# Only the first scatter group of a pair waits for TensorE's count

## The chip, the core and the metric

The kernel runs on one core of a Trainium2 chip. The engines are TensorE (PE), VectorE (DVE), ScalarE (ACT), GpSimd (POOL) and SyncE (SP), each with its own ordered list of instructions; sixteen DMA engines move data. The metric is the device time of one execution in microseconds; lower is better. The kernel before took 10546.78 us in the median of 3 runs (10500.81 to 10546.99).

## What is computed

Two layers over a graph of 12,500 nodes with 256 features and 212,500 edges, in float32. Cut to what bears on the changed stage:

```python
edge_index = jnp.stack([src, dst])
xn = _layernorm(x, axis=-1)
x = x + gcn_residual(xn, edge_index, edge_weight, ...) + linear_attention(xn, ...)
x = x + moe(_layernorm(x, axis=-1), router_w, w1, b1, w2, b2)   # 8 experts, top 2 combined
...
# moe: every expert is applied to every token
for e in range(8):
    h = gelu(tokens @ w1[e] + b1[e])
    y = h @ w2[e] + b2[e]
    out = out + combine[:, e:e+1] * y
# second layer: graph sum over the same edges, sorted anew, attention, feed-forward, slice attention
```

## The kernel before

The program is a row of stages, each with its own semaphores and a barrier behind it. The stage in question is `finish_layer0` (L1269). It takes the 100 tiles of 125 nodes in 50 pairs (`NP = 50`, `TE = 2` tiles each) and does, for each pair, the end of the graph layer and of the attention (the "front"), the 8 experts, and the norm and keys that the second layer needs (the "back").

The order is written out by hand. Every engine walks through 32 slots a pair; in slot n TensorE does one up product (`up`, L1955, tokens times a half of `w1[e]`, 4 matmuls with their weight loads) or one down product (`down`, L1965), and the front of the next pair and the back of the pair before are dealt out over the same slots. TensorE adds one to a semaphore behind each product. `up_done` counts the up products: 16 a pair, and product c of expert e in pair i brings it to i*16 + e*2 + c + 1. ScalarE waits for it and applies gelu (L1836), and adds to `up_kept`; TensorE's down product waits for that and adds to `dn_done`; VectorE waits for `dn_done` and adds the weighted result to `acc` (L1556), and adds to `dn_kept`, which TensorE awaits before it writes that bank again. There are two banks for up and two for down. So TensorE can run a few products ahead and then needs the others' counts, and these need its own. By the code TensorE gives 56 such counts a pair: 16 up, 16 down and 24 of front and back.

Beside this, GpSimd does a job that has nothing to do with the experts: it puts the edge records in a new order for the second layer. The records lie as 1,700 rows of 125 (`RPP = 34` rows a pair), and each row is one indirect DMA of 128 lanes with 12 bytes each, from `rec` to `sorted_recs` (L1472). Nobody in this stage reads `sorted_recs`; the next stage does, behind the barrier. SyncE loads `rec` and `pos` two pairs ahead (L1393, L1394) into four buffers, when GpSimd's `share_done` says that the buffer is free; the same SyncE queue loads `x` (L1431) and stores `x2` and `table1` (L1440, L1441).

GpSimd's 34 scatters of pair i are dealt into 8 groups (`NE = 8`; sizes 4, 4, 4, 5, 4, 4, 4, 5). Before group g it waits until `up_done` is at least (i-1)*16 + 2g + 1, that is until TensorE has done the first up product of expert g in pair i-1. Pair 0 has no such wait. Behind group 1 it waits until all scatters of the pair before have landed and gives SyncE `share_done`.

Of the kernel before, what the change touches and what calls it, by code (L numbers as in the profile page):

```python
# [1268 lines left out]
def finish_layer0(nc, k):  # L1269
# [11 lines left out]
    with ExitStack() as ctx:  # L1281
# [69 lines left out]
        S = Shared()  # L1351
# [30 lines left out]
        def by_fours(eng, run):  # L1382

            run(0, 0, 0)
            with eng.Fori(0, (NP - 2) // 4) as m:
                for q in range(1, 5):
                    run(m * 4 + q, q % 4, m + q // 4)
            run(NP - 1, (NP - 1) % 4, (NP - 1) // 4)
# [66 lines left out]
        @block.gpsimd  # L1455
        def _(eng):
            eng.memset(rec[:, :, :, :], 0).then_inc(spare_lanes, 1)
            for ring in range(4):
                eng.iota(pos[:, ring, :], [[LANES - P, RPP]], base=P * k.ROWS + ring % 2 * RPP * (LANES - P) - P,
                         channel_multiplier=1).then_inc(spare_lanes, 1)  # L1460
            eng.sem_inc(S.share_done, 1)

            def run(i, ring, turn):
                n = ring % 2
                eng.wait_ge(rec_in[ring], turn * 32 + 32)
                eng.nop(nofuse=True)
                for group in range(NE):
                    if not isinstance(i, int) or i > 0:
                        eng.wait_ge(S.up_done, (i - 1) * 16 + group * 2 + 1)
                        eng.nop(nofuse=True)  # L1470
                    for r in range(group * RPP // NE, (group + 1) * RPP // NE):
                        eng.indirect_dma_start(  # L1472
                            out=k.sorted_recs, out_offset=bass.IndirectOffsetOnAxis(ap=pos[:, ring, r:r + 1], axis=0),
                            in_=rec[:, ring, r, :], in_offset=None).then_inc(scattered[n], 16)
                    if group == 1 and (not isinstance(i, int) or i > 0):

                        eng.wait_ge(scattered[1 - n], (turn * 2 + (ring + 1) // 2) * (16 * RPP))
                        eng.sem_inc(S.share_done, 1)

            by_fours(eng, run)  # L1480
            for n in range(2):
                eng.wait_ge(scattered[n], 16 * RPP * (NP // 2))
                eng.nop(nofuse=True)
# [1848 lines left out]
```

## Time and profile before

| | us |
|---|---|
| median of 3 runs | 10546.78 |
| the profiled execution, its own time | 10519.44 |
| its span, first to last instruction | 10517.9 |
| TensorE matmul busy | 7714.1 (73%) |
| VectorE busy | 6440.3 (61%) |
| GpSimd busy | 5497.1 (52%) |
| ScalarE busy | 1737.1 (17%) |
| scatters, L1472, 1700 of them | 1717.7 busy |
| gathers of the graph sums, L879, 3600 of them | 3474.5 busy |

A reader should know: busy time is that of instructions, not of their waits. A matmul's end is modelled from its start. "Releaser" is what the profile takes to have ended an engine's idle time; "issue" means that nothing visible was waited for, and "remote" that the wait ended by a semaphore event for which the profile shows no instruction ending at that moment. A DMA_INDIRECT on POOL is the time in which GpSimd writes the descriptors, not that of the transfer. The granted TensorE clock was 0.82 of full speed over the span.

### The profile page before, as it was taken

The numbers are of one execution on the slowest core, as the hardware profiler recorded it, in microseconds if no ns is written. First come the engines' busy times: TensorE is split into PE (matmuls) and PEld (weight loads), VectorE is DVE, ScalarE is ACT, GpSimd is POOL, SyncE is SP. The second block draws the span as 40 slices with busy tenths as digits, with TensorE's granted clock in tenths as the row PEclk, the third lists the DMA queues.
The fourth block names the chain that finished last, engine by engine and source line by source line (L and its number), as shares of the span: only waits on it lengthen the run. The fifth ranks groups of instructions, "written<-read, shape, count | busy, mean of one in ns | idle before, by whom it ended". The sixth has DMA issues, their size and how long they took to land. (4 is left out here: it accounts for less than half of the span.)

```text
span 10517.9 us, 141328 instructions
## 1 busy us (share of the span) xinstructions
PE 7714.1 (73%) x33929; PEld 5693.3 (54%) x33929; DVE 6440.3 (61%) x22399; ACT 1737.1 (17%) x3475; POOL 5497.1 (52%) x5833
## 2 busy tenths in 40 slices
PE   4845565665665668888888888677777777777998
PEld 3634444444444446666666666455555555554667
DVE  5755555665655656666666666465565565555983
ACT  1110000000000013333333333111001101110221
POOL 2235555555555555665655666366565666654002
PEclk7767777777777779999999999788888888887999
DMA  1022222222222210000000000233232333322446
GB/s 48 29 87 80 79 82 82 82 83 80 84 83 81 82 56 15 16 16 15 17 16 15 17 16 15 58 91 93 89 91 89 93 93 90 92 86 77 127 114 195
DMA packets 451199, 724.74 MB, mean 69 GB/s; under 512 B 144672, under 2 KB 304613, under 8 KB 450193
## 3 DMA queue, kind: packets, MB, share of 16 engines
q0 software_dynamic: 235408, 493.09, 16.5%
q1 hardware_dynamic: 215180, 224.92, 7.4%
q14 instruction: 451, 3.69, 0.1%
q10 hardware_dynamic: 130, 2.55, 0.1%
q8 instruction: 30, 0.49, 0.0%
HBM read 611.64 MB, written 108.50 MB: 68 GB/s over the span
## 5 line engine op out<-in xcount | busy, mean ns | idle before, releaser
L879 POOL DMA_INDIRECT sum_gathered<-table,sum_idx x3600 | 3474.5, 965 | 2485.5 <-PE sum_agg_res L943 1180.7
L943 PE MATMUL sum_agg_res<-sum_gathered,sum_lay 125*125 125x256 f32 x7200 | 2480.2, 486 | 1315.7 <-DVE sum_lay L909 507.8
L943 PEld LDWEIGHTS sum_agg_res<-sum_gathered,sum_lay 125*125 125x125 f32 x7200 | 1576.2, 235 | 1961.2 <-DVE all_sums L928 1122.8
L928 DVE TENSOR_TENSOR all_sums<-all_sums,sum_agg_res 125x256 f32 x3600 | 1511.4, 420 | 1426.6 <-PE sum_agg_res L943 699.7
L1472 POOL DMA_INDIRECT sorted_recs<-fin_rec,fin_pos x1700 | 1717.7, 1010 | 1131.3 <-PE fin_ps_up L1961 481.3
L909 DVE TENSOR_SCALAR sum_lay<-all_lane,sum_dloc_now,sum_w_now 125x125 f32<-125x125 f32 x3612 | 1284.3, 356 | 53.2 <-issue 37.8
L1969 PE MATMUL fin_ps_dn<-fin_w,fin_hidden 128*125 128x256 f32 x3200 | 916.0, 422 | 84.6 <-DVE fin_acc L1556 60.3
L1961 PE MATMUL fin_ps_up<-fin_tokens_T,fin_w 128*128 128x250 f32 x3200 | 859.3, 396 | 73.0 <-ACT fin_hidden L1836 67.3
L1969 PEld LDWEIGHTS fin_ps_dn<-fin_w,fin_hidden 128*125 128x125 f32 x3200 | 633.6, 209 | 236.4 <-issue 134.5
L1556 DVE SCALAR_TENSOR_TENSOR fin_acc<-fin_ps_dn,fin_comb,fin_acc 125x256 f32<-125x256 f32 x800 | 381.4, 481 | 617.9 <-remote 355.8
L1961 PEld LDWEIGHTS fin_ps_up<-fin_tokens_T,fin_w 128*128 128x128 f32 x3200 | 603.0, 201 | 192.6 <-ACT fin_hidden L1836 99.2
L1836 ACT ACTIVATE fin_hidden<-fin_ps_up,fin_b 128x250 f32<-128x250 f32 x800 | 367.0, 470 | 1125.4 <-PE fin_ps_up L1961 590.3
L1043 DVE CUSTOM_DVE_ANT_0 sum_junk<-sum_src_hot,sum_ps_rank 125x100 f32<-125x100 bf16 x1700 | 335.9, 253 | 238.1 <-DMA table<-all_sums 226.5
L1124 PE MATMUL sum_ps_rank<-sum_src_hot,sum_edges_after 125*125 125x100 bf16 x1700 | 209.8, 257 | 349.1 <-DVE sum_rank_now L1043 275.3
L1033 DVE TENSOR_TENSOR sum_src_hot<-sum_lane,steps_src_tile 125x400 bf16<-125x400 bf16 x425 | 243.8, 574 | 350.1 <-DMA table<-all_sums 279.0
L1124 PEld LDWEIGHTS sum_ps_rank<-sum_src_hot,sum_edges_after 125*125 125x125 bf16 x1700 | 191.0, 172 | 455.2 <-DVE sum_rank_now L1043 334.1
L2527 PE MATMUL sum_ps_C<-sum_x_T,sum_w 128*128 128x500 f32 x800 | 397.2, 621 | 40.9 <-ACT sum_x_T L2457 29.0
L2536 PE MATMUL sum_ps_A<-sum_w,sum_low 128*125 128x256 f32 x1600 | 381.1, 381 | 15.2 <-ACT sum_low L2462 11.4
L2536 PEld LDWEIGHTS sum_ps_A<-sum_w,sum_low 128*125 128x125 f32 x1600 | 301.7, 189 | 140.1 <-issue 86.5
L865 ACT COPY sum_idx<-steps_src_p 128x36 int32 (+1 forms) x102 | 22.6, 222 | 1577.1 <-PE sum_agg_res L943 1104.5
L2462 ACT ACTIVATE sum_low<-sum_ps_C,sum_b 128x500 f32<-128x500 f32 x200 | 135.2, 677 | 842.0 <-PE sum_ps_C L2527 513.9
L1100 ACT ACTIVATE sum_exp_key<-sum_key_less_max 125x256 f32<-125x256 f32 x100 | 41.6, 416 | 1357.2 <-issue 689.6
(534 smaller groups left out, 10964.8 us busy)
## 6 DMA issues: line engine op xcount, KB each, us to landing
sum_gathered<-table,sum_idx POOLq DMA_INDIRECT x3600
sorted_recs<-fin_rec,fin_pos POOLq DMA_INDIRECT x1700
slice_weights<-slices_sw SPq DMA_DIRECT2D x50, 480.0 KB
out_sw<-slice_weights SPq DMA_DIRECT2D x50, 480.0 KB
deg_x_tiles<-in_x SPq DMA_DIRECT2D x100, 125.0 KB
sum_x_tiles<-in_x SPq DMA_DIRECT2D x100, 125.0 KB
fin_x<-in_x SPq DMA_DIRECT2D x100, 125.0 KB
x<-fin_acc SPq DMA_DIRECT2D x100, 125.0 KB
```

What stands on the lines that cost most here:

```text
L879: eng.indirect_dma_start(out=self.rows[:, s % self.RING, :], out_offset=None, in_=self.table, in_offset=bass.IndirectOffsetOnAxis(ap=self. ...
L909: ins = eng.tensor_scalar(self.lay[:, g % 2, l, :], k.lane[0:P, 0:P], self.dl[:, s:s + 1], self.wl[:, s:s + 1], ALU.is_equal, ALU.mult)
L928: eng.tensor_tensor(sums, sums, res, ALU.add).then_inc(self.added, 1)
L943: eng.matmul(self.res[s % self.RES][:, 0, :], self.lay[:, g % 2, l, :], self.rows[0:P, s % self.RING, :], start=True, stop=True).then_inc( ...
L1124: mm = eng.matmul(ps_rank[:, q, :], upper[:], hot[:, slot(b), q, :], start=False, stop=False, skip_group_check=True)
L1472: eng.indirect_dma_start(out=k.sorted_recs, out_offset=bass.IndirectOffsetOnAxis(ap=pos[:, ring, r:r + 1], axis=0), in_=rec[:, ring, r, :] ...
L1556: eng.scalar_tensor_tensor(out=acc[:, n, j, :], in0=ps_dn[j][:, :], scalar=comb[:, n, j, e:e + 1], in1=acc[:, n, j, :], op0=ALU.mult, op1= ...
L1836: eng.activation(hid[:, e % 2, c, :], ps_up[c][:, :], ACT.Gelu, bias=b1[:, c, e:e + 1])\
L1961: mm = eng.matmul(ps_up[c][:, :], w1[:, e, m, c * H2:(c + 1) * H2], xtT[:, n, m, :, :], start=(m == 0), stop=(m == 1))
L1969: mm = eng.matmul(ps_dn[j][:, :], hid[:, e % 2, m, j * P:(j + 1) * P], w2[:, e, m, :], start=(m == 0), stop=(m == 1))
L2527: mm = eng.matmul(ps_C[u % 2][:, 0:T], w1[:, m, u * 128:(u + 1) * 128], xT[:, m, :], start=(m == 0), stop=(m == 1))
L2536: mm = eng.matmul(ps_A[j // 2][0:P, (j % 2) * D:(j % 2 + 1) * D], hid[:, u % 2, j * P:(j + 1) * P], w2[:, u, :], start=(u == 0 and j % 2 = ...
```

## The change

For pairs 1 to 49 only group 0 waits for `up_done`, with the value (i-1)*16 + 1, as before; groups 1 to 7 have neither wait nor nop. Everything else, the wait for the landings of the pair before and `share_done` behind group 1 among it, is as it was.

```diff
@@ -1465,8 +1465,8 @@
                 eng.wait_ge(rec_in[ring], turn * 32 + 32)
                 eng.nop(nofuse=True)
                 for group in range(NE):
-                    if not isinstance(i, int) or i > 0:
-                        eng.wait_ge(S.up_done, (i - 1) * 16 + group * 2 + 1)
+                    if group == 0 and (not isinstance(i, int) or i > 0):
+                        eng.wait_ge(S.up_done, (i - 1) * 16 + 1)
                         eng.nop(nofuse=True)
                     for r in range(group * RPP // NE, (group + 1) * RPP // NE):
                         eng.indirect_dma_start(
```

## Rows read from the trace of the kernel before

**Rows 1.** The page, part 1: busy us, share of the span, instructions.
```profile
PE 7714.1 (73%) x33929; PEld 5693.3 (54%) x33929; DVE 6440.3 (61%) x22399; ACT 1737.1 (17%) x3475; POOL 5497.1 (52%) x5833
```
**Rows 2.** Windows, 4400 to 5000 us: length, busy PE, PEld, DVE, ACT, POOL, clock, DMA.
```profile
4400.00:5000.00 600.00, 508.41 (x2192) 398.31 (x2191) 388.59 (x1497) 226.05 (x451) 363.84 (x359) 0.92 0.07 16
```
**Rows 3.** Groups by line, 4400 to 6200 us: busy, mean ns, idle before and releasers.
```profile
L1472 POOL DMA_INDIRECT sorted_recs<-fin_rec,fin_pos x1081 | 1092.5, 1011 | 709.3 <-PE fin_ps_up L1961 294.9 <-issue 281.4 <-remote 133.0
```
**Rows 4.** Waits, 4400 to 6200 us: total us, times, longest us.
```profile
ACT fin_hidden L1836 <- remote: 313.4, 56, 8.5
POOL sorted_recs L1472 <- PE fin_ps_up L1961: 294.9, 134, 7.7
...
DVE fin_acc L1556 <- remote: 217.8, 83, 7.0
```
**Rows 5.** Timeline, ACT (start, us, operation), first and last of 50 pairs.
```profile
3811.65 0.57 ACT L1844 COPY fin_xn_sum_T<-fin_ps_A 128x500 f32<-128x500 f32 x1 [49.73 <-issue]
...
6584.14 0.57 ACT L1844 COPY fin_xn_sum_T<-fin_ps_A 128x500 f32<-128x500 f32 x1
```
**Rows 6.** Timeline, POOL: first and last scatter of pair 0, first of pair 1.
```profile
3784.43 1.02 POOL L1472 DMA_INDIRECT sorted_recs<-fin_rec,fin_pos  x1 [3.30 <-DMA fin_pos<-pos_d]
...
3826.16 0.96 POOL L1472 DMA_INDIRECT sorted_recs<-fin_rec,fin_pos  x1 [0.30 <-issue]
3857.41 0.96 POOL L1472 DMA_INDIRECT sorted_recs<-fin_rec,fin_pos  x1 [30.29 <-PE fin_ps_up L1961]
```
**Rows 7.** Timeline, PE, the front of pair 0.
```profile
3812.42 1.94 PE L1997 MATMUL fin_ps_C<-fin_w_gcn,fin_xn_sum_T 128*125 128x256 f32 x4
3814.15 1.91 PE L1997 MATMUL fin_ps_A<-fin_w_q,fin_xn_sum_T 128*125 128x256 f32 x4
3815.85 1.24 PE L1997 MATMUL fin_ps_B<-fin_w_gcn,fin_xn_sum_T 128*125 128x256 f32 x4
...
3836.60 0.65 PE L2016 MATMUL fin_ps_B<-all_ident,fin_query 125*128 125x125 f32 x2 [14.82 <-DVE fin_query L1634]
```
**Rows 8.** Timeline, DVE and ACT, that read those products.
```profile
3819.16 0.48 DVE L1614 SCALAR_TENSOR_TENSOR fin_gcn<-fin_ps_C,all_dinv,fin_b_gcn 125x256 f32<-125x256 f32 x1 [7.02 <-remote]
3828.95 0.42 DVE L1620 TENSOR_REDUCE fin_qmax<-fin_ps_A 125x8 f32<-125x256 f32 x1 [9.30 <-remote]
...
3832.48 0.48 DVE L1614 SCALAR_TENSOR_TENSOR fin_gcn<-fin_ps_B,all_dinv,fin_b_gcn 125x256 f32<-125x256 f32 x1 [2.64 <-remote]
...
3837.29 0.37 ACT L1875 COPY fin_query_T<-fin_ps_B 128x250 f32<-128x250 f32 x1 [2.09 <-PE fin_ps_B L2016]
```
**Rows 9.** Timeline, all engines, a burst of eight scatters inside the stage.
```profile
4994.53 0.95 POOL L1472 DMA_INDIRECT sorted_recs<-fin_rec,fin_pos  x1 [7.02 <-PE fin_ps_up L1961]
...
4997.11 1.03 PE L1969 MATMUL fin_ps_dn<-fin_w,fin_hidden 128*125 128x256 f32 x4
...
5000.57 1.01 PE L1961 MATMUL fin_ps_up<-fin_tokens_T,fin_w 128*128 128x250 f32 x4
...
5003.36 0.96 POOL L1472 DMA_INDIRECT sorted_recs<-fin_rec,fin_pos  x1 [0.30 <-issue]
5004.56 0.48 DVE L1556 SCALAR_TENSOR_TENSOR fin_acc<-fin_ps_dn,fin_comb,fin_acc 125x256 f32<-125x256 f32 x1 [6.25 <-remote]
```
**Rows 10.** Timeline, DVE, inside the burst of 4747.90 to 4759.08.
```profile
4753.69 0.17 DVE L1700 COPY fin_logit<-fin_ps_A 125x8 f32<-125x8 f32 x1 [0.92 <-remote]
...
4756.54 0.48 DVE L1556 SCALAR_TENSOR_TENSOR fin_acc<-fin_ps_dn,fin_comb,fin_acc 125x256 f32<-125x256 f32 x1 [2.21 <-remote]
```
**Rows 11.** Windows, a burst of 13 scatters; columns as in rows 2.
```profile
3869.70:3887.10 17.40, 13.78 (x59) 10.83 (x57) 9.70 (x37) 6.33 (x12) 13.73 (x13) 0.90 0.08 20
```
**Rows 12.** Timeline, PE: behind a stall, and first and last of pair 49.
```profile
5048.76 2.03 PE L1961 MATMUL fin_ps_up<-fin_tokens_T,fin_w 128*128 128x250 f32 x4 [5.67 <-ACT fin_hidden L1836]
...
6629.73 1.85 PE L1961 MATMUL fin_ps_up<-fin_tokens_T,fin_w 128*128 128x250 f32 x8
...
6662.94 3.66 PE L1969 MATMUL fin_ps_dn<-fin_w,fin_hidden 128*125 128x256 f32 x16
```
**Rows 13.** Waits of SP's queue, 4400 to 6200 us, the longest in total.
```profile
SPq L1440 <- DVE fin_next_norm L1575: 625.5, 20, 34.1
```

## Prediction, made before the changed kernel was run

> **What bounds the kernel now.** I read the page first: one core, a span of 10517.9 us, no engine saturated over the whole of it, TensorE the busiest at 73% [rows 1]. The changed line belongs to one stage of many, so the next view is the busy time by stretches. The experts' stage runs from about 3780 to 6690 us. Inside it TensorE is busy 508 of 600 us, VectorE 389, GpSimd 364, and the sixteen DMA engines 7% [rows 2]. TensorE's ordered list of work therefore sets the pace, but it stands still for 15% of the time. The first copy of each pair's transposes on ScalarE gives the period: 3811.65 for pair 0, 6584.14 for pair 49, so (6584.14 - 3811.65) / 49 = 56.6 us a pair [rows 5].
>
> GpSimd's scatters look harmless by their busy time. One takes 1.01 us in the mean, with 0.3 us of issue behind it [rows 3]; 34 of them are about 43 us of the 56.6. Nobody in the pair's arithmetic waits for a scatter. SyncE's longest waits are for VectorE's rows, not for the count that GpSimd gives it [rows 13]. So at first sight neither the gates nor their removal can matter.
>
> The waits view says otherwise, by one odd word. ScalarE's gelu waited 313 us and VectorE's expert sum 218 us for something "remote", while GpSimd waited 295 us for TensorE's `ps_up` [rows 4]. A remote wait here is one where the matmul had long ended by the profile and its count had still not come. The timelines show when that happens.
>
> - Pair 0 is a case without gates in the kernel before (`i > 0` is false there). GpSimd issues its 34 scatters from 3784.43 to 3827.12 (3826.16 + 0.96), 1.26 us apart, and then rests for 30.29 us [rows 6]. TensorE's three products end by the profile at 3814.36, 3816.06 and 3817.09 [rows 7]. VectorE, idle and waiting for exactly these, gets them at 3819.16, 3828.95 and 3832.48 [rows 8]: 4.8, 12.9 and 15.4 us late, the second one 1.8 us after the last scatter ended. In GpSimd's rest the same handover takes nothing: a transpose that ends at 3837.25 is copied at 3837.29 [rows 7, 8].
> - Inside the stage a burst of eight scatters runs from 4994.53 to 5004.32. TensorE's down product ends at 4998.14; VectorE gets it at 5004.56, 6.4 us late and only after GpSimd has stopped [rows 9].
>
> That this is GpSimd's doing and not the reverse is what pair 0 decides: there the burst ends by its own count and waits for nobody, and the counts still come when it is over. The first counts after a rest pass freely. In the burst that begins at 4994.53 the first late one is that of 4998.14, so some 4 to 5 us are free [rows 9].
>
> The Trainium skill speaks against this reading. Its page "SBUF — State Buffer", section "SBUF: two separate sides", says that on the engine side only the port pair of GpSimd and VectorE is contended and that PE and ACT never wait for anyone; by that rule the scatters can't touch TensorE and the time would stay at 10547 us. The rule is on SBUF's ports, though, and the rows above are on counts. Its page "Perfetto Trace Analysis", section "Per-instruction lifecycle", says that the time a semaphore takes to become visible lies outside the window shown for an instruction; by that the delay has to be read from the start of the waiting engine, and the trace agrees (6.4 us there against 0.04 us in the rest).
>
> **The change part by part.** Removed: for each of pairs 1 to 49, seven waits on `up_done` and seven nops on GpSimd. Their own issue is hidden today, since the removed gates are where GpSimd waits. Nothing is added. Moved: scatter groups 1 to 7, 30 DMAs a pair on GpSimd's queue, to right behind group 0, as is the wait for the pair before (satisfied long before) with the count for SyncE behind group 1. No other queue is passed. The number and size of the transfers stays.
>
> What it does to GpSimd: each pair becomes one burst of 34 scatters, as in pair 0: 42.7 us [rows 6], taken as 43. The gate of group 0 opens with the first up product of a pair, so the burst starts with TensorE's pair and is followed by a rest until the next one.
>
> What it does to TensorE: by the code a pair has 56 counts of TensorE that others wait for (16 up, 16 down, 24 of the fronts and backs). Without scatters they run at 0.88 us each: the last pair's 42 (no front part there) go from 6629.73 to 6666.60 [rows 12]. Thus an undisturbed pair would take 56 x 0.88 = 49.3 us. In a burst of 43 us:
> - the first 5 us are free: 5 counts [rows 9];
> - in the other 38 us counts trickle. Lower bound: 1 in 12.8 us, from 3814.36 to 3827.12 [rows 7, 8], 0.08 a us, so 3 counts. Upper bound: between 4751.6 and 4759 VectorE gets three, two of them the rows of 4753.69 and 4756.54, 0.4 a us, so 15 counts [rows 10]. I take 0.25, the middle, since pair 0 is the shape that the change makes but a single case: 9.5 counts;
> - TensorE runs some 4 products ahead of its missing counts before it stands (from the late one of 4997.11 seven products start before it stands at 5003.3, the first three of which the free part feeds [rows 9]): 4.
>
> That is 18.5 of 56. The other 37.5 follow in the rest: 37.5 x 0.88 = 33 us. The release after the last scatter takes 1.9 us (3827.12 to 3828.95), and TensorE comes back at half its clock: four up matmuls take 2.03 us after a stall of 5.67 us against 1.01 us at full clock [rows 9, 12]; about 2 us a pair. Sum: 43 + 1.9 + 33 + 2 = 80 us a pair against 56.6, +23.4. Pairs 1 to 49 of the scatters lie beside TensorE's pairs 0 to 48, so 49 x 23.4 = +1147 us. From the profiled execution's own time, 10519.4 us (span 10517.9 and 1.5 around it), this gives 11666; the median of the runs is 27 us above that execution, so **11690 us**.
>
> The bounds of this term: with 0.08 counts a us, 44 are left, 38.7 us, 85.6 a pair, +1421, 11970. With 0.4: 32 left, 75 a pair, +906, 11480. With nothing passing and no running ahead: 51 left, 91.8 a pair, +1725, 12270. The likeliest case's own range is 11300 to 12270. What takes the place of the removed waits is no wait of GpSimd but longer ones of VectorE and ScalarE for TensorE. GpSimd itself finishes earlier in each pair, which nobody uses.
>
> **The rivals.**
> - *Mild.* Counts pass in a long burst at a rate near today's. For it: one burst of 13 scatters in the stage, 3869.7 to 3887.1, in which TensorE still starts 59 matmuls in 17.4 us, 3.4 a us [rows 11] against 3.65 in the stage [rows 2]. At that pace a pair of 207 matmuls does 146 in the burst, the other 61 take 14.5 us at the undisturbed rate, and the pair takes 59.4 us: +2.8, +140 us. Against it: that burst grew long because a gate was found open, that is because counts came through. Between this and the likeliest case I price it at 59.4 to 68 us, +140 to +560: 10690 to 11110, 10910 in the middle.
> - *Nothing.* The late counts have a cause outside the scatters, and GpSimd only waits for the same thing. Then 10547, as GpSimd's work isn't on anybody's path. Against it stand pair 0 and its rest.
> - *Faster.* Each burst delays TensorE once, when it has gone on for some 4 us, and the delay heals by itself after about 5 us. Today a pair has about five bursts (its 34 scatters in groups), with the change one. Then a single stall of 3 to 4 us is left: 49.3 + 3.5 = 53 us, -3.6, -176 us: 10370. It decides if counts flow again in the middle of a long burst; pair 0, with nothing between 3819.16 and 3828.95, speaks against it.
>
> **How the numbers follow.** Chances: likeliest 0.65, mild 0.17, nothing 0.10, faster 0.06, something else 0.02. A measurement of this kernel tells about 0.5% from no change. Faster by over 0.5%: 0.06. Within: 0.11 (nothing, and the least of mild). Slower: 0.83. The range from 10700 to 12300 holds the likeliest case and nearly all of mild, about 8 in 10.
>
> **What would show it.** In the changed kernel GpSimd should show 34 scatters at 1.26 us and then one idle stretch of some 35 us a pair, released by `ps_up`. TensorE's busy share in the stage should fall from 85% to about 60%, with "remote" the largest releaser of VectorE's expert sum and ScalarE's gelu, several times today's. Right behind each burst several waits should end together. The stages before 3780 us and behind this one should be unchanged in length. The prediction is wrong in its root if TensorE is as busy as now inside the bursts, and wrong in its size if the pair is not between 75 and 92 us.

## The result, and the profile after

The changed kernel takes 11924.01 us in the median of 4 runs (11913.38 to 11936.3); beside it on the same chip the kernel before takes 10546.89 (4 runs, 10500.81 to 10567.56). The ratio is 1.131 (95% interval 1.1285 to 1.134): **1377 us slower**. The prediction was 11690 (10700 to 12300), slower with a chance of 0.83.

The profiled execution took 11936.3 us, its span 11934.7. First the page's part 1 and its line for the scatters (busy and mean ns of one; then the idle time before them and its releasers), and below it the window of rows 2, with the same columns.

```profile
PE 7840.6 (66%) x33929; PEld 5753.7 (48%) x33929; DVE 6435.4 (54%) x22399; ACT 1750.0 (15%) x3475; POOL 5426.1 (45%) x5833
...
L1472 POOL DMA_INDIRECT sorted_recs<-fin_rec,fin_pos x1700 | 1633.6, 961 | 2572.2 <-PE fin_ps_up L1961 2066.6
```

```profile
4400.00:5000.00 600.00, 352.53 (x1442) 269.54 (x1442) 254.25 (x980) 153.19 (x301) 231.15 (x241) 0.74 0.05 11
```

Every engine has its instructions of before [rows 1], and nearly its busy time; what grew is idle time. TensorE does 1442 matmuls in 600 us instead of 2192 [rows 2]: its busy share in the stage falls from 85% to 59% and its granted clock from 0.92 to 0.74.

How the pair looks, from GpSimd's timeline (start, us, operation, idle time before it with its releaser): the first two scatters and the last of one burst, and the first of the next.

```profile
5044.71 0.96 POOL L1472 DMA_INDIRECT sorted_recs<-fin_rec,fin_pos  x1 [42.47 <-PE fin_ps_up L1961]
5045.98 0.96 POOL L1472 DMA_INDIRECT sorted_recs<-fin_rec,fin_pos  x1 [0.30 <-issue]
...
5086.46 0.96 POOL L1472 DMA_INDIRECT sorted_recs<-fin_rec,fin_pos  x1 [0.30 <-issue]
5129.94 0.96 POOL L1472 DMA_INDIRECT sorted_recs<-fin_rec,fin_pos  x1 [42.51 <-PE fin_ps_up L1961]
```

34 scatters in 42.71 us (5044.71 to 5087.42), 1.26 us apart, then 42.5 us of rest: 85.2 us from burst to burst, against 56.6 a pair before [rows 5]. The expert sum's rows close the count (durations, then its first to last start), of the changed kernel and of the kernel before:

```profile
L1556 DVE SCALAR_TENSOR_TENSOR fin_acc<-fin_ps_dn,fin_comb,fin_acc x800: 465/483/486, 3863.8 to 8066.5; 125x256 f32<-125x256 f32 x160
```

```profile
L1556 DVE SCALAR_TENSOR_TENSOR fin_acc<-fin_ps_dn,fin_comb,fin_acc x800: 468/484/486, 3863.0 to 6666.6; 125x256 f32<-125x256 f32 x160
```

4202.7 us against 2803.6: 1399 us more for 49 bursts, 28.6 us each.

The windows of this burst, of its rest and of the burst's last 31 us (columns as in rows 2):

```profile
5044.71:5087.42 42.71, 14.80 (x59) 11.23 (x57) 6.92 (x28) 3.03 (x6) 32.66 (x34) 0.63 0.07 13
5087.42:5129.94 42.52, 36.45 (x149) 27.69 (x150) 29.51 (x113) 18.80 (x37) 0.01 (x2) 0.81 0.03 8
5056.00:5087.42 31.42, 6.16 (x14) 3.95 (x14) 1.82 (x4) 0.47 (x1) 24.01 (x25) 0.50 0.03 4
```

```profile
5048.99 0.58 ACT L1844 COPY fin_xn_sum_T<-fin_ps_B 128x500 f32<-128x500 f32 x1 [1.57 <-remote]
...
5050.63 1.01 PE L1961 MATMUL fin_ps_up<-fin_tokens_T,fin_w 128*128 128x250 f32 x4
5051.48 1.02 PE L1997 MATMUL fin_ps_B<-fin_w_gcn,fin_xn_sum_T 128*125 128x256 f32 x4
...
5053.30 0.48 DVE L1556 SCALAR_TENSOR_TENSOR fin_acc<-fin_ps_dn,fin_comb,fin_acc 125x256 f32<-125x256 f32 x1 [3.13 <-remote]
...
5058.98 0.48 DVE L1614 SCALAR_TENSOR_TENSOR fin_gcn<-fin_ps_C,all_dinv,fin_b_gcn 125x256 f32<-125x256 f32 x1 [5.20 <-remote]
5059.52 2.07 PE L1997 MATMUL fin_ps_C<-fin_w_q,fin_xn_sum_T 128*125 128x256 f32 x4 [6.17 <-issue]
...
5063.97 0.48 DVE L1556 SCALAR_TENSOR_TENSOR fin_acc<-fin_ps_dn,fin_comb,fin_acc 125x256 f32<-125x256 f32 x1 [4.50 <-PE fin_ps_dn L1969]
5070.99 0.42 DVE L1620 TENSOR_REDUCE fin_qmax<-fin_ps_A 125x8 f32<-125x256 f32 x1 [6.54 <-remote]
...
5072.40 1.91 PE L1969 MATMUL fin_ps_dn<-fin_w,fin_hidden 128*125 128x256 f32 x4
...
5080.82 0.47 ACT L1836 ACTIVATE fin_hidden<-fin_ps_up,fin_b 128x250 f32<-128x250 f32 x1 [31.25 <-remote]
5090.62 0.48 DVE L1614 SCALAR_TENSOR_TENSOR fin_gcn<-fin_ps_B,all_dinv,fin_b_gcn 125x256 f32<-125x256 f32 x1 [18.75 <-remote]
...
5091.16 0.68 PE L2016 MATMUL fin_ps_B<-all_ident,fin_next_norm 125*128 125x125 f32 x2 [16.84 <-DVE fin_gcn L1614]
```

The product into `ps_B` ends at 5051.48 + 1.02 = 5052.50. VectorE has waited for it since 5071.87 (18.75 us) and gets it at 5090.62: 38.1 us after its end, 3.2 us after the last scatter ended. By the code this `gcn` step waits for TensorE's count and for nothing else. The counts come in the order in which TensorE gave them, each later than the one before. Seven products that end between 5048.21 and 5053.35 are read 5.1, 9.9, 14.0, 20.2, 29.2, 38.1 and 39.4 us after their ends (at 5053.30, 5058.98, 5063.97, 5070.99, 5080.82, 5090.62 and 5092.76).

A product's end is modelled, so one has to ask whether the products themselves were late. TensorE works in order, and it started later products at 5059.52 and 5072.40, long before 5090.62: it is the count that is late. Nor are all counts late. VectorE's `gcn` ends at 5058.98 + 0.48 = 5059.46, and TensorE, which waits for it, starts at 5059.52, in the middle of the burst. It is the pattern of pair 0 [rows 6 to 8], now in every pair. The waits of 4400 to 6200 us (total us, times, longest us):

```profile
POOL sorted_recs L1472 <- PE fin_ps_up L1961: 894.9, 21, 44.3
ACT fin_hidden L1836 <- remote: 797.7, 35, 37.0
DVE fin_gcn L1614 <- remote: 434.2, 32, 20.9
...
DVE fin_qmax L1620 <- remote: 196.3, 38, 9.8
```

Gelu's remote wait is 2.5 times that of rows 4, over fewer pairs. The expert sum's is not: it fell from 217.8 to 76.7 us, and VectorE's remote waits now lie ahead of `gcn` and `qmax`.

### The profile page after: what moved, and what is told of

Read it like the earlier page. It is cut to its first block and busy times, and to the rows that moved or that the text cites. A ratio compares the mean times of both kernels' runs of the same rounds, so it can differ in the third digit from the quotient of the medians.

```text
span 11934.7 us, 140649 instructions
## 1 busy us (share of the span) xinstructions
PE 7840.6 (66%) x33929; PEld 5753.7 (48%) x33929; DVE 6435.4 (54%) x22399; ACT 1750.0 (15%) x3475; POOL 5426.1 (45%) x5833
## 5 line engine op out<-in xcount | busy, mean ns | idle before, releaser
L1472 POOL DMA_INDIRECT sorted_recs<-fin_rec,fin_pos x1700 | 1633.6, 961 | 2572.2 <-PE fin_ps_up L1961 2066.6
L1961 PE MATMUL fin_ps_up<-fin_tokens_T,fin_w 128*128 128x250 f32 x3200 | 893.4, 411 | 8.2 <-ACT fin_hidden L1836 8.2
L2016 PE MATMUL fin_ps_B<-all_ident,fin_next_norm 125*128 125x125 f32 x100 | 33.5, 437 | 809.2 <-issue 440.1
L1614 DVE SCALAR_TENSOR_TENSOR fin_gcn<-fin_ps_B,all_dinv,fin_b_gcn 125x256 f32<-125x256 f32 x50 | 24.2, 484 | 908.0 <-remote 828.8
```

The lines of the kernel that those rows point to most:

```text
L1472: eng.indirect_dma_start(out=k.sorted_recs, out_offset=bass.IndirectOffsetOnAxis(ap=pos[:, ring, r:r + 1], axis=0), in_=rec[:, ring, r, :] ...
L1961: mm = eng.matmul(ps_up[c][:, :], w1[:, e, m, c * H2:(c + 1) * H2], xtT[:, n, m, :, :], start=(m == 0), stop=(m == 1))
```

## The experiments

The chips turned out to differ: the kernel before took 10538 to 10560 us on some ("the 10550 chips"; the prediction and the result are from such) and 8579 to 8590 us on others ("the 8590 chips"). The comparisons are always with the kernel before on the same chip. The texts of expectation name theories by letters. A is the prediction's own: the scatters hold TensorE's counts up; A1 says by any burst of over some 5 us, A2 only when they follow one another too fast, so that a backlog builds. B: what counts is GpSimd's tie to TensorE's progress, or the number of gates. C: GpSimd being busy is what delays them, scatters or not. D: it depends on the chip. E: it doesn't, and the change costs its 1377 us everywhere. F: the many tiny writes to memory with their completions do it, whoever issues them. G: any DMA that GpSimd issues does it. H: only the indirect form does. "Pair" is always the distance of the first and last of ScalarE's 50 copies into `xn_sum_T`, divided by 49, as for rows 5. It is 84.4 us for the changed kernel, a little under the 85.2 us above, as the first of the 49 distances is short (47.0 us).

### First comparison, on an 8590 chip

**Fewer gates: the kernel before with the gates of groups 0, 2, 4 and 6 only.**

```diff
-                    if not isinstance(i, int) or i > 0:
+                    if group % 2 == 0 and (not isinstance(i, int) or i > 0):
                         eng.wait_ge(S.up_done, (i - 1) * 16 + group * 2 + 1)
```

> The kernel before with only every second gate (groups 0, 2, 4, 6), so bursts of 8 or 9 scatters. Theory A: the delay grows with the length of a burst beyond its first 4 to 5 us, so between the kernel before and the changed one but much nearer to before: 10650 to 11000 us. Theory B (the number of gates matters in proportion): half way between, about 11200 us.

Measured: 8590.83 against 8589.64 us (13 runs), ratio 1.0001 (0.9991 to 1.0011). No change, and a pair takes 43.35 us. Its window of 400 us in the stage, and the copies that give the pair (durations, then first to last start):

```profile
3800.00:4200.00 400.00, 393.88 (x1891) 319.31 (x1890) 331.48 (x1283) 200.52 (x394) 308.69 (x300) 1.00 0.09 21
```

```profile
L1844 ACT COPY fin_xn_sum_T<-fin_ps_A x50: 575/575/576, 3038.0 to 5162.2; 128x500 f32<-128x500 f32 x50
```

The numbers expected were for a 10550 chip, and this kernel never ran on one. What the run shows is something else: GpSimd is busy with scatters for 309 of 400 us, and TensorE is busy for 394 of them at the full clock. On this chip scatters beside TensorE cost it next to nothing, and no engine has a remote wait from 3800 to 5000 us.

**Landings: the changed kernel, where groups 1 to 7 wait until the stage's own scatters have landed.**

```diff
+                    if group > 0:
+                        eng.wait_ge(scattered[n], (turn * 2 + ring // 2) * (16 * RPP) + 16 * (group * RPP // NE))
+                        eng.nop(nofuse=True)
```

> The changed kernel, with a wait of GpSimd for the landing of its own scatters ahead of groups 1 to 7 in place of the removed waits for TensorE's count. Theory A (a running stream of GpSimd DMAs holds back TensorE's counts, and any pause of the stream lets them through): seven pauses of some 2 us a pair, no burst longer than 5 scatters; TensorE almost undisturbed, GpSimd's own cycle of 43 + 7 x 2 = 57 us sets the pair; 10400 to 10700 us. Theory B (what counts is that GpSimd is tied to TensorE's progress, not the pause): as the changed kernel, 11900 us or more.

Measured: 9267.97 us, ratio 1.0786 (1.0768 to 1.0804), 56.0 us a pair. **Breaks: the changed kernel with three memsets on GpSimd, 1.5 us together, before each of the groups 1 to 7** (the counter `filled` only keeps them in order; the scratch tile is read by nobody).

```diff
+                    if group > 0:
+                        for part in range(3):
+                            at = (turn * 4 + ring) * 21 + (group - 1) * 3 + part
+                            if not isinstance(at, int) or at > 0:
+                                eng.wait_ge(filled, at)
+                                eng.nop(nofuse=True)
+                            eng.memset(idle_fill[:], 0.0).then_inc(filled, 1)
```

> The changed kernel with three memsets of 128x384 on GpSimd ahead of groups 1 to 7: GpSimd stays busy, but issues no DMA for some 2 us. Theory A (the DMA stream is the cause): the pauses work as those of e1_land do, 10400 to 10800 us. Theory C (GpSimd being busy at all is the cause): no help, 12000 us or more.

Measured: 9017.95 us, ratio 1.05 (1.0483 to 1.0518), 51.2 us a pair. **Spacing: the changed kernel with a memset of 128x64 behind every scatter.** They then start 1.29 us apart, and not 1.5 to 1.6 as expected.

```diff
                             in_=rec[:, ring, r, :], in_offset=None).then_inc(scattered[n], 16)
+                        at = (turn * 4 + ring) * RPP + r
+                        if not isinstance(at, int) or at > 0:
+                            eng.wait_ge(filled, at)
+                            eng.nop(nofuse=True)
+                        eng.memset(idle_fill[:], 0.0).then_inc(filled, 1)
```

> The changed kernel with one small memset (128x64) behind every scatter, so the 34 scatters come about 1.5 to 1.6 us apart and not 1.26, in one unbroken row. Theory A1 (the stream must stand still for about 2 us before counts pass): as the changed kernel or worse, since the row is longer: 12000 to 12600 us. Theory A2 (a backlog builds up because the scatters come a little too fast; a bit more room drains it): 10400 to 10900 us.

Measured: 8666.4 us, ratio 1.009 (1.0073 to 1.0107), 44.6 us a pair. None of the three has a remote wait in its stage. They are slower for a reason of their own. The waits of the landing kernel, of GpSimd, of VectorE and of SyncE's queue (3800 to 5000 us):

```profile
POOL sorted_recs L1475 <- DMA sorted_recs<-fin_rec,fin_pos: 343.6, 142, 6.1
DVE fin_acc L1665 <- DMA table<-fin_next_norm: 287.4, 40, 15.3
```

```profile
SPq L1393 <- POOLq L1481: 1042.8, 21, 50.9
```

SyncE stands for 1043 of 1200 us before `load_records`, waiting for GpSimd's `share_done`; in the kernel with fewer gates that wait is 70 us. The later loads of `x` and the stores stand behind it in the same queue. VectorE waits 287 us for the stores of the pair before (`table<-fin_next_norm`) to end, since only then may it write that half of `acc` again.

What sets the time here can be read from the scatters: the time from the first to the last of the 1,700, with a fiftieth of it as GpSimd's list of a pair, and the growth of both over the kernel with fewer gates.

| kernel | first to last scatter, us | a pair | more than fewer gates | the kernel's time, more |
|---|---|---|---|---|
| fewer gates | 3010.2 to 5293.9 = 2283.7 | 45.7 | | |
| spacing | 3015.3 to 5369.6 = 2354.3 | 47.1 | 70.6 | 75.6 |
| breaks | 3015.1 to 5723.8 = 2708.7 | 54.2 | 425.0 | 427.1 |
| landings | 3021.9 to 5984.6 = 2962.7 | 59.3 | 679.0 | 677.1 |

The time grows by what GpSimd's list grows. That list is longer than 34 x 1.26 = 42.8 us a pair, mostly since some scatters take up to 3.2 us, and longer than TensorE's 43.35 us: already with fewer gates the last scatter starts 56 us after the last expert sum (5293.9 against 5238.3). So on such a chip GpSimd is the bound of the stage, a little ahead of TensorE. TensorE gets some way ahead of it and is then held by `share_done`. Whatever is added to GpSimd's list is added to the time, and the late counts of the theory don't occur.

### Second comparison: the two kernels again, on a 10550 chip

> The changed kernel itself, beside the kernel before on one chip. In the four runs before this one TensorE's counts were never late and the kernel before took 8590 us, not 10547. Theory D (how late TensorE's counts come under a stream of GpSimd DMAs is a property of the chip or its state that day): where the kernel before takes about 8590 us, the changed one is the same within 0.5%, 8560 to 8640; where it takes about 10550, the changed one takes about 11920. Theory E (the change costs its 1377 us everywhere): slower by over 1000 us wherever it runs.

> The kernel before, unchanged, for its profile on the same chip. Theory D: on a chip where it takes about 8590 us no count of TensorE is late in any stage, the experts' stage takes 43 to 44 us a pair, and the sums' stages are shorter as well; where it takes 10550, the profile is that of the kernel before as it stands.

Measured: 11911.46 against 10559.89 us (7 runs), ratio 1.13 (1.127 to 1.1329), 84.4 us a pair; the kernel before once more 10550.05 and 57.1 us a pair. The effect is there again with its size, as theory D wants it of such a chip, and theory E too; the two differ only on an 8590 chip. The two kinds of chip can now be set side by side where their programs do the same. Of the kernel before on the 10550 chip: the window in the stage, the page's line of the graph sums' gathers, and the expert sums (first to last start); and then the last two of the kernel with fewer gates on the 8590 chip.

```profile
4400.00:5000.00 600.00, 506.52 (x2144) 392.76 (x2143) 380.18 (x1456) 224.73 (x451) 359.26 (x354) 0.91 0.07 16
```

```profile
L879 POOL DMA_INDIRECT sum_gathered<-table,sum_idx x3600 | 3472.2, 964 | 2487.0 <-PE sum_agg_res L943 1180.3
```

```profile
L1556 DVE SCALAR_TENSOR_TENSOR fin_acc<-fin_ps_dn,fin_comb,fin_acc x800: 468/484/486, 3874.5 to 6705.0; 125x256 f32<-125x256 f32 x160
```

```profile
L879 POOL DMA_INDIRECT sum_gathered<-table,sum_idx x3600 | 3496.5, 971 | 1164.9 <-issue 1053.8
```

```profile
L1556 DVE SCALAR_TENSOR_TENSOR fin_acc<-fin_ps_dn,fin_comb,fin_acc x800: 468/479/485, 3072.5 to 5238.3; 125x256 f32<-125x256 f32 x160
```

A gather takes GpSimd 0.96 to 0.97 us and an expert sum VectorE 0.48 us on both. The two profiled spans differ by 10548.5 - 8589.1 = 1959 us: 787 us before the first scatter (3797.3 against 3010.2), 586 us from the first to the last (2869.4 against 2283.7), and 587 us behind it. TensorE's part of the experts' stage alone differs by more (2830.5 against 2165.8 us, 665), as on the 8590 chip the stage ends with the scatters. Outside this stage GpSimd's idle time before the gathers is what stands out (2487.0 against 1164.9 us, 1322 more); 1180.3 us of it end with TensorE's `sum_agg_res` on the 10550 chip and 110.0 on the other.

### Third comparison, on another 10550 chip

**Breaks again**, the very kernel of above.

> The changed kernel with three memsets (1.5 us in all) on GpSimd ahead of groups 1 to 7, once more, for a chip on which TensorE's counts come late. GpSimd stays busy, but its row of DMAs breaks off for 1.8 us each 4 or 5 scatters. Where the kernel before takes about 10550 us: theory A (the running stream of DMAs is the cause, and a pause lets the counts through) gives 10300 to 10800; theory C (GpSimd being busy is the cause) 12000 or more. Where before takes 8590: 9018 again, as GpSimd's own cycle is the limit there.

Measured: 10403.42 us (10398.37 to 10408.48) against 10537.68 (3 runs), ratio 0.9875 (0.9825 to 0.9925): 1.2% under the kernel before, from 2 runs against 3, and some 1500 us under the changed kernel on the two other 10550 chips (it didn't run on this one). A pair takes 53.5 us. Copies and waits (4400 to 6200 us):

```profile
L1853 ACT COPY fin_xn_sum_T<-fin_ps_A x50: 568/576/577, 3812.2 to 6434.3; 128x500 f32<-128x500 f32 x50
```

```profile
ACT fin_hidden L1845 <- PE fin_ps_up L1970: 371.5, 253, 6.6
...
ACT fin_hidden L1845 <- remote: 204.8, 50, 12.0
```

**Wide spacing: a memset of 128x384 behind every scatter**, without any longer break; otherwise the edit of the spacing kernel.

> The changed kernel with one memset of 128x384 (0.5 us) behind every scatter: 34 scatters in one row, 1.6 us apart in place of 1.26, and no longer stop. Where before takes about 10550: theory A1 (the stream must stand still for some 2 us) gives 12000 to 12600, the row being 12 us longer; theory A2 (a backlog from scatters that come too fast) gives 10400 to 11000. Where before takes 8590: about 9150, GpSimd's cycle of 55 us setting the pair.

Measured: 10412.67 us (10401.31 to 10424.03), ratio 0.9884 (0.9829 to 0.9939), again 2 runs, 52.0 us a pair. The scatters in GpSimd's timeline, the waits of 4400 to 6200 us, and SyncE's:

```profile
4499.40 0.96 POOL L1474 DMA_INDIRECT sorted_recs<-fin_rec,fin_pos  x1 [0.17 <-POOL fin_idle_fill L1481]
4500.36 0.43 POOL L1481 MEMSET fin_idle_fill<- 128x384 f32 x1
4500.96 0.96 POOL L1474 DMA_INDIRECT sorted_recs<-fin_rec,fin_pos  x1 [0.16 <-POOL fin_idle_fill L1481]
```

```profile
ACT fin_hidden L1843 <- PE fin_ps_up L1968: 762.6, 380, 16.3
DVE fin_acc L1669 <- DMA table<-fin_next_norm: 318.8, 66, 12.4
```

```profile
SPq L1395 <- POOLq L1485: 1504.0, 33, 48.8
```

These two settle four points. Neither has any of the gates 1 to 7, and the counts pass: B falls. GpSimd is busy for 526 of 600 us with the wide spacing (4400 to 5000 us), against 231 in the changed kernel, and the counts pass: C falls. The unbroken stream of 34 scatters, 1.56 us apart, doesn't hold them either: A1 falls and A2 stands, a stream hurts when its scatters come too close. With the breaks gelu still waits 205 us for remote counts, against 798 in the changed kernel, which also shows that this chip is of the kind that has them; with the wide spacing no engine has a remote wait. There the bound is GpSimd's own list, 2749.8 us for the 1,700 scatters or 55.0 a pair, and SyncE waits for `share_done` for 1504 of 1800 us. TensorE's pace is GpSimd's now, but for the start that it has.

One thing is not separated: each memset comes with a wait and a nop of its own, so the room between two scatters and this wait are one change. The spacing kernel, which has the same waits with only 0.03 us more room, would tell, and never ran on a 10550 chip.

**Where in a scatter the cause lies.** Two kernels do no scatter in the stage: all 1,700 follow in a stage of their own behind it, which adds some 2,200 us to the time, so that only the stage is to be read. In their place 34 plain stores a pair of 125 rows of 12 bytes go from `rec` to a scratch tensor. In the first SyncE issues them, in the second GpSimd, in one row behind the gate of group 0. The loads of `rec` and `pos` are gone from the stage with the scatters. Each kernel ran once.

```diff
+                    for r in range(RPP):
+                        eng.dma_start(tiny[n, r], rec[0:P, ring, r, :]).then_inc(scattered[n], 16)
...
-                        eng.indirect_dma_start(
-                            out=k.sorted_recs, out_offset=bass.IndirectOffsetOnAxis(ap=pos[:, ring, r:r + 1], axis=0),
-                            in_=rec[:, ring, r, :], in_offset=None).then_inc(scattered[n], 16)
```

> No scatter in the experts' stage: they follow in a stage of their own behind it (about 34 x 50 x 1.27 = 2160 us more). In their place SyncE issues 34 small stores a pair (125 rows of 12 bytes, to a scratch buffer) in one row. Where before takes about 10550: theory F (completions of any small DMAs hold back TensorE's counts) gives a pair of 65 us or more in the experts' stage; theory G (only DMAs whose descriptors GpSimd writes do) an undisturbed pair of 42 to 50 us.

> As e6_hw, but GpSimd issues the 34 small stores as plain DMAs, not indirect ones, in one row behind the gate of group 0. Where before takes about 10550: theory G (whatever DMA's descriptors GpSimd writes) gives the changed kernel's 84 us a pair, less if a plain DMA is issued faster; theory H (the indirect form alone) an undisturbed pair of 42 to 50 us.

Measured: 12064.3 and 12080.25 us, on the chip of the third comparison. The stage of SyncE's stores:

```profile
4400.00:5000.00 600.00, 577.54 (x2734) 468.19 (x2733) 473.65 (x1859) 290.47 (x569) 0.00 (x0) 0.98 0.22 18
```

```profile
L1883 ACT COPY fin_xn_sum_T<-fin_ps_A x50: 576/576/577, 3804.4 to 5990.6; 128x500 f32<-128x500 f32 x50
```

and of GpSimd's, with half a burst of them in its timeline:

```profile
4400.00:5000.00 600.00, 581.51 (x2784) 471.02 (x2783) 484.71 (x1900) 292.13 (x578) 230.97 (x444) 1.00 0.11 19
```

```profile
L1892 ACT COPY fin_xn_sum_T<-fin_ps_A x50: 575/575/577, 3821.9 to 5974.1; 128x500 f32<-128x500 f32 x50
```

```profile
4421.48 8.86 POOL L1526 DMA_DIRECT2D tiny<-fin_rec  x17 [25.15 <-PE fin_ps_up L2009]
```

Pairs of 44.6 and 43.9 us, TensorE busy 96 to 97% of the time, on a chip of the kind on which the kernel before takes 56.6 and 57.1 us for the same pair. No engine has a remote wait there. F and G fall: neither tiny writes with as many completions as the scatters have, nor stores issued by GpSimd, even 0.52 us apart, hold a count. The loads that are gone too can't be the cause, as the wide spacing has them and no late count. What is left is H, the indirect form. What in it (the list of offsets, the scattered addresses, a lane or three more) was not taken apart.

### Fourth comparison, which fell on another 8590 chip

**Half the width (128x192, scatters 1.40 us apart), and the narrow spacing again.**

> The changed kernel with a GpSimd memset of 128x192 behind every scatter, half the width of the wide version (128x384, scatters 1.56 us apart, 52.0 us a pair). From the two sizes run so far (128x64: 1.29 us apart, 128x384: 1.56) the scatters should start about 1.40 us apart, so GpSimd's own work for a pair is 34 x 1.40 = 47.6 us and a little. Theory A2 (counts pile up only while scatters come faster than some rate between 1.26 and 1.56 us) leaves two results open: if 1.40 us is wide enough, the pair is set by GpSimd at 48 to 50 us, 10200 to 10330 us, under the kernel before and under the wide version; if it is not, counts come late inside the burst and the pair is 60 to 84 us, 10900 to 11900. Theory A1 (any burst of over 5 us delays counts whatever its spacing) gives the latter. On a chip like the one that takes 8590 us for the kernel before, neither shows: pair of about 48 us, 8800 us.

> The kernel of e4_space (the changed kernel with a GpSimd memset of 128x64 behind every scatter, scatters 1.29 us apart instead of 1.26) on a chip that takes some 10550 us for the kernel before. GpSimd spends 34 x 1.29 = 44 us a pair. Theory A2 as a threshold: 0.03 us more room a scatter hardly changes the backlog, the pair stays at 75 to 85 us, 11400 to 11950 us. A2 as a balance (each count needs a fixed room, and what is missing per scatter is small): most of the delay is gone, 50 to 65 us a pair, 10300 to 11000. Theory D (depends on the chip): on a chip like the one that takes 8590 us it repeats 8666 us.

Measured against 8578.77 us (7 runs): 8805.95, ratio 1.0267 (1.025 to 1.0284), and 8652.33, ratio 1.0089 (1.0073 to 1.0106). Pairs of 47.4 and 44.5 us; GpSimd's lists take 2505.3 and 2349.4 us in all, 50.1 and 47.0 a pair. The windows of the two, in this order:

```profile
3800.00:4200.00 400.00, 371.68 (x1673) 294.99 (x1672) 302.31 (x1141) 176.20 (x349) 347.07 (x551) 0.95 0.09 19
```

```profile
3800.00:4200.00 400.00, 390.44 (x1863) 315.06 (x1862) 332.70 (x1268) 196.74 (x388) 340.57 (x571) 1.00 0.09 21
```

It is the result expected for such a chip, and a second chip on which a nearly unbroken stream 1.29 us apart leaves TensorE busy 98% of the time. The question for which they were made, how little room is enough on a 10550 chip, stays open between 1.26 and 1.56 us. The changed kernel itself never ran on an 8590 chip, so what the change costs there isn't shown, and E isn't refuted by its own test. The nearest is this narrow spacing, 0.9% above the kernel before and without a remote wait, which speaks against E.

## Why the prediction was right, and where it was off

**Root and direction: right.** The stall is TensorE's counts held up while GpSimd scatters, and the gates were what broke the stream up. On the 10550 chips the changed kernel loses 13% in both comparisons; giving GpSimd breaks by memsets instead of gates takes the whole loss back and 1.2% more. But two limits were missing from the reasoning. It is the close stream that does it, not scatters as such, and late counts showed on some chips only. The prediction read one chip's trace and spoke of the kernel.

**Burst: right.** 42.7 us against 43.

**What passes in the burst: mis-sized.** Forecast were 18.5 of 56 counts: 5 in the first 5 us, 9.5 in the other 38 us (0.25 a us) and 4 of running ahead. In the burst shown 5 are read in the first 5 us, though the first late one is already among them (it ends at 5047.34 and is copied at 5048.99). Behind them come 5 in 38 us (5053.30 to 5080.82), 0.13 a us, nearer to the bound from pair 0 (0.08) than to the middle that was taken. TensorE had run 6 ahead when the burst ended. That is 16, as 59 of 208 matmuls are.

**The pace in the rest: mis-sized the other way.** 0.88 us a count was read from pair 49, which has no front beside it. An undisturbed pair takes 43.9 us, 0.78 a count, not 49.3 in all. The two errors nearly cancel, which is luck: more counts were left than forecast, and each went faster.

**Release and clock: both too small.** The rest of 42.5 us comes apart like this: 149 matmuls at the undisturbed pace of 600 / 2784 = 0.216 us are 32.1 us, forecast 33. From the last scatter's end at 5087.42 to TensorE's start at 5091.16 are 3.7 us, forecast 1.9; rows 8 already had a count that came 5.4 us after pair 0's burst (3832.48 against 3827.12). A matmul takes 36.45 / 149 = 0.245 us of busy time against 581.51 / 2784 = 0.209, at a granted clock of 0.81 against 1.00: 5.3 us, forecast 2. What is left, 1.4 us, isn't assigned. So the rest was 33 + 1.9 + 2 = 37 in the forecast and is 42.5; the pair 80 and is 85.2. 49 x 5.2 = 255 us is about what the median missed by (11924 against 11690, 234 us).

**A slip in the bounds.** For 0.4 counts a us the prediction gives 11480. Its own sum, 10519.4 + 906 + 27, is 11452; the range of 10700 to 12300 doesn't hang on it.

**The signs named beforehand.** TensorE's share 60%: 59%. 34 scatters 1.26 us apart and one rest released by `ps_up`: so it is, of 42.5 us instead of 35. Several waits that end right behind the burst: `gcn` at 5090.62, gelu at 5092.76. The remote waits of gelu: 2.5 times. Of the expert sum: wrong, they fell from 217.8 to 76.7 us, since VectorE goes by the order of its own list and most of its waiting falls to the front's `gcn` and `qmax`. The kernel's earlier stages are unchanged (first copy at 3814.7 against 3811.65). Behind the stage the span is 17 us longer (3820.9 against 3803.9 us from the first gather of `plan_rec_g`, L292, to the end), which stays unexplained.

**The rivals.** "Nothing" may come true on the 8590 chips, where no version showed a late count, but for another reason than its own (a cause outside the scatters); the changed kernel didn't run there. "Mild" and "faster" asked that counts flow in a long burst; 14 matmuls in 31 us answer both. The Trainium skill's rule that PE and ACT wait for nobody (page "SBUF — State Buffer", section "SBUF: two separate sides") is not refuted, as it speaks of SBUF's ports: with scatters 77% of the time beside it, TensorE is busy 98% on the 8590 chip. It just doesn't tell the time of a kernel whose engines hand over by counts.

**What gates and breaks do.** The kernel before was not at its best on its chip. A gate waits for the very count that the scatters hold up, so it can open late, 295 us of waiting in rows 4, and gives GpSimd a rest only then; this is argued from the rows, and no run took it apart. A break that doesn't ask TensorE puts some 10 us a pair on GpSimd's list, and the pair still ends at 53.5 against 56.6. On the 8590 chips the same break costs 5%. No version that ran beats the kernel before on both kinds of chip.

## What to carry to other kernels

A wait that looks like mere coupling may be what throttles a stream: before it is removed, look in the trace for a stretch where it is absent (here pair 0) and read how late the other engines' handovers come there. If a stream has to be throttled, do it by its own clock and not by a count that it delays itself, and leave no more room than the engine behind it can spare. And before a stall is put down to the program, run it on a second chip.

## What the runs showed of the hardware

- The same kernel takes 10538 to 10560 us on at least two chips and 8579 to 8590 us on two others. A gather, a scatter and an expert sum last the same on both (0.96 to 0.97, 0.96 and 0.48 us). Of the difference of 1959 us, 586 lie in this stage, where it is TensorE's counts that come late, and 1373 before and behind it, where GpSimd's idle time ahead of the gathers is 1322 us longer. That the gathers' share has the same cause is inferred from GpSimd's waits for TensorE there; no run spaced the gathers. Each chip served in one comparison, so a lasting property of it can't be told from a state that it was in.
- On the 10550 chips, under 34 scatters 1.26 us apart, TensorE's counts come in order and one in 5 to 10 us (5053.30 to 5090.62). One came 38 us late (5052.50 to 5090.62), 3.2 us after the stream's end. VectorE's count to TensorE in the same burst took 0.06 us (5059.46 to 5059.52).
- 0.3 us more room for each scatter (1.56 us apart) leaves no remote wait; 1.5 us for every four or five leaves gelu 205 us of them in 1800 us, against 798 in the changed kernel.
- Plain stores issued by GpSimd, 0.52 us apart, or by SyncE, do nothing of the kind there. Why one kind of chip shows it and the other doesn't is open.
